# Shorter leads, a hand-written order of the last stage, and a last row added and normalised in another way, in a one-core kernel of two graph layers

## The reference, cut to what matters

```
N, F = 8192, 64                                     # adj is 8192 x 8192, float32 (268 MB)
x_drop = x * (u >= 0.1) / 0.9
x      = layernorm(x + adj @ x_drop)                # layer 1, rows of 64
proj   = tanh(|x|) * x / (|x| + 1e-8)               # row norms
s      = adj @ proj                                 # layer 2, the same adj
n      = clip(|s|, 0, 0.999)
out    = layernorm(x + (arctanh(n) * s / (n + 1e-8)) @ kernel + bias)
```

## Time and profile before

| | before |
|---|---|
| median of 3 runs | 947.8 us (947.53 to 947.82) |
| the profiled execution | 946.4 us |
| its span, first to last instruction | 944.2 us |
| PE busy | 898.7 us (95%) |
| DVE, POOL, ACT busy | 283.0, 56.9, 53.2 us |
| queue of the `adj`, `x` and `u` loads | 355.49 MB, 93.4% of the DMA engines' span |
| granted clock of TensorE, mean | 0.994 |

### The profile page before, as it was taken

One profiled execution on the slowest core, in us unless ns is written; L12 is line 12 of the kernel. 1 busy time (PEld: TensorE's weight loads), 2 busy tenths in 40 slices (PEclk: granted clock), 3 DMA queues, 4 the chain that ended last, 5 costly groups with the idle time before them and its releaser, 6 DMA issues.

```text
span 944.2 us, 10549 instructions
## 1 busy us (share of the span) xinstructions
PE 898.7 (95%) x4224; PEld 322.4 (34%) x4224; DVE 283.0 (30%) x1046; ACT 53.2 (6%) x138; POOL 56.9 (6%) x49
## 2 busy tenths in 40 slices
PE   5669999999999999999999999999999999999993
PEld 1113333333333333333333444444444444443331
DVE  1134574322314130304040221203121030336644
ACT  0000110000000000000000000000000000013322
POOL 0000000000000000000000000000000000003322
PEclk9999999999999999999999999999999999999997
DMA  9999999999999999997979998997989979899992
GB/s 369 414 421 420 421 421 420 421 422 421 421 421 421 421 417 422 380 423 258 424 237 413 390 363 320 341 423 283 407 290 370 422 269 362 336 423 421 421 422 108
DMA packets 53328, 358.35 MB, mean 380 GB/s; under 512 B 6305, under 2 KB 8353, under 8 KB 10401
## 3 DMA queue, kind: packets, MB, share of 16 engines
q1 hardware_dynamic: 50544, 355.49, 93.4%
q10 hardware_dynamic: 2736, 2.20, 0.7%
HBM read 355.57 MB, written 2.10 MB: 379 GB/s over the span
## 4 chain that ended last, share of the span: by engine, by line
PE 83%; DMA 7%; DVE 3%; SPq 2%; ACT 2%; POOL 1%; issue 1%; ACTq 0%; POOLq 0%; DVEq 0%
PE sums_both L629 38%; PE sums_first L583 20%; PE sums_part L592 16%; DMA ring<-adj_dram 7%; PE sums_part L583 4%; PE sums_both L611 3%; PE sums_part L611 3%; SPq L313 1%; ACT xres L363 1%; POOL rooted L330 1%; DVE stats L425 1%; SPq L309 1%; DVE y L541 1%; SPq L308 0%; DVE mv L428 0%
## 5 line engine op out<-in xcount | busy, mean ns | idle before, releaser
L629 PE MATMUL sums_both<-ring,feats 128*64 128x512 f32 x1696 | 370.3, 592 | 0.5 <-DMA ring<-adj_dram 0.5
L583 PE MATMUL sums_first<-ring,feats 128*64 128x512 f32 x1088 | 246.6, 599 | 28.4 <-DMA ring<-adj_dram 28.4
L629 PEld LDWEIGHTS sums_both<-ring,feats 128*64 128x64 f32 x1696 | 136.7, 137 | 228.0 <-issue 226.0
L592 PE MATMUL sums_part<-ring,feats 128*64 128x512 f32 x880 | 193.3, 593 | 0.0
L583 PEld LDWEIGHTS sums_first<-ring,feats 128*64 128x64 f32 x1088 | 78.8, 138 | 189.3 <-issue 140.1
L435 DVE TENSOR_TENSOR row_saved<-sums_both,row_saved 64x512 f32<-64x512 f32 x15 | 10.2, 683 | 349.3 <-ACT row_saved L383 349.2
L592 PEld LDWEIGHTS sums_part<-ring,feats 128*64 128x64 f32 x880 | 66.9, 137 | 119.0 <-issue 118.2
L340 POOL TENSOR_TENSOR rooted<-base,power 128x8 f32<-128x8 f32 x16 | 27.8, 1735 | 795.7 <-DVE base L462 795.7
L492 DVE TENSOR_TENSOR support<-sums_part,support 128x512 f32<-128x512 f32 x36 | 24.9, 692 | 139.2 <-PE sums_part L592 139.1
L583 PE MATMUL sums_part<-ring,feats 128*64 128x512 f32 x208 | 48.5, 595 | 2.8 <-DMA ring<-adj_dram 2.8
L383 ACT COPY row_saved<-sums_first 64x512 f32<-64x512 f32 x16 | 9.3, 580 | 600.4 <-PE sums_first L583 600.4
(11 more groups left out here) (64 smaller groups left out, 236.1 us busy)
## 6 DMA issues: line engine op xcount, KB each, us to landing
ring<-adj_dram SPq DMA_DIRECT2D x335, 1024.0 KB, 12.9
xres<-x_dram SPq DMA_DIRECT2D x8, 256.0 KB, 17.0
support<-u_dram SPq DMA_DIRECT2D x8, 256.0 KB, 16.8
out_dram<-xres ACTq DMA_DIRECT2D x16, 128.0 KB, 7.5
selw<-selector_dram ACTq DMA_DIRECT2D x1, 32.0 KB, 3.4
selw<-weight_dram ACTq DMA_DIRECT2D x1, 32.0 KB, 3.7
bias_sb<-bias_dram ACTq DMA_DIRECT2D x1, 32.0 KB, 6.1
```

The lines of the kernel that those rows point to most:

```text
L583: last = nc.tensor.matmul(bank[at:at + F], feats[:, c * TB + t, which, :], ring[:, slot, t, :], start=start and t < 2, stop=stop and t >= ...
L592: last = nc.tensor.matmul(bank[F * g:F * g + F], feats[:, c * TB + t, 1, :], ring[:, slot, t, :], start=start and t == 0, stop=stop and t ...
L629: last = nc.tensor.matmul(sums_both[r % 2][layer * F:layer * F + F], feats[:, c * TB + t, layer, :], ring[:, slot, t, :], start=begin and ...
```

## The change

It has these parts:

1. `LEAD` goes from 7 to 6. It counts in every row, and in the run of parts after the last row.
2. `EARLY_RUN` goes from 3 to 4: in row 1, `early` steps and steps of row 1 alternate in runs of four instead of three.
3. `HELD[2]` goes from 4 to 5: block (2, 6) is held and not read a second time. There are 334 loads instead of 335.
4. The order of the groups in the last stage is a list (`FINISHED`), and a second list (`GAPS`) says how many blocks stand between `finish` steps. The groups come in the same order as before. Some `finish` steps stand one or two blocks elsewhere.
5. For the last row (5), POOL clears the half of `support` that belonged to row 4 once row 4 was projected. VectorE then adds the whole 128 x 512 bank to it in one instruction, instead of two of 64 x 512, and the projection sums over 128 rows.
6. The last row's normalisation is shared: two of its four tiles on ScalarE as before, two on VectorE. Each half has its own store, from ACT's and from SP's queue.
7. `x` and `u` of a chunk come in one transfer of 512 KB instead of two of 256 KB, into a common tile `rows_in`. `support` shares the bytes of `u` as before.

```diff
-LEAD = 7
-EARLY_RUN = 3
-FINISH_EVERY = 3
-FINISH_LAG = 1
-HELD = [4, 4, 4, 3, 5, 4, 3, 4, 6, 5, 4, 3, 3, 2, 2, 1]
+LEAD = 6
+EARLY_RUN = 4
+HELD = [4, 4, 5, 3, 5, 4, 3, 4, 6, 5, 4, 3, 3, 2, 2, 1]
+FINISHED = [(14, 15), (12, 13), (8, 9), (10, 11), (0, 1), (2, 3), (6, 7), (4,), (5,)]
+GAPS = [7, 4, 4, 4.5, 4, 8, 5, 5, 5]
...
-            if ended and since >= FINISH_EVERY and now - ended[0][1] >= FINISH_LAG:
-                order.append(("finish", ended.pop(0)[0]))
-                since = 0
+            if ended < g and since >= GAPS[ended]:
+                order.append(("finish", groups[ended][0]))
+                ended, since = ended + 1, 0
...
-        xres = sb("xres", [P, NT, F])
-        support = sb("support", [P, NB // 2, BS])
+        rows_in = sb("rows_in", [P, 2, NT, F])
+        xres, keep = rows_in[:, 0], rows_in[:, 1]
...
-                    sp.dma_start(xres[:, t, :], x[:, t, :]).then_inc(chunk_loaded[chunk], 16)
-                    sp.dma_start(keep[:, t, :], u[:, t, :]).then_inc(chunk_loaded[chunk], 16)
+                    sp.dma_start(rows_in[:, :, t, :], xu[:, chunk]).then_inc(chunk_loaded[chunk], 16)
...
+                    if k == mate_done:
+                        pool.wait_ge(rows_projected, k + 1)
+                        nc.gpsimd.memset(support[half(final ^ 1), final // 2], 0.0).then_inc(mate_cleared, 1)
...
+                if k == len(groups) - 1:
+                    tiles = slice(final * TB, final * TB + TB // 2)
+                    for i in range(TB // 2):
+                        last = nc.scalar.activation(xres[:, final * TB + i, :], y_of[k % 2][:, i, :], ACT.Identity,
+                                                    scale=rooted[:, 0, i:i + 1], bias=shift[:, i:i + 1])
+                    last.then_inc(out_ready, 1)
+                    act.wait_ge(out_ready, rows_before(k) + 1)
+                    act.dma_start(out[:, tiles, :], xres[:, tiles, :]).then_inc(out_stored, 16)
...
-                if len(rows) == 2:
+                if n == final_part:
+                    dve.wait_ge(mate_cleared, 1)
+                if len(rows) == 2 or n == final_part:
                     total = support[:, rows[0] // 2]
                     V.tensor_tensor(total, bank[:], total, ALU.add).then_inc(part_added, 1)
...
+            dve.wait_ge(deviation_ready, 2 * k + 1)
+            for i in range(TB // 2, TB):
+                last = V.tensor_scalar(xres[:, final * TB + i, :], y_of[k % 2][:, i, :], mv[:, i, 0:1],
+                                       rooted[:, 0, i:i + 1], ALU.subtract, ALU.mult)
+            last.then_inc(final_halved, 1)
...
+                    for t in range(TB if rows == (final,) else 0):
+                        last = nc.tensor.matmul(projected[finished % 2][0][:, t, :],
+                                                support[:, final // 2, t * P:(t + 1) * P],
+                                                selw[:], start=True, stop=True)
```

More of the change, by code:

```diff
@@ L126, in work_order @@
     order += reread(LEAD, last) + column(last)
-    pairs = sorted(range(NB // 2), key=lambda p: 2 * NB - reread_to[2 * p] - reread_to[2 * p + 1])
     groups = []
-    for pair in pairs[:-1]:
+    for together in FINISHED:
         steps = []
         while True:
-            rows, low, high = behind(pair, NB)
-            if not rows:
+            low = min(reread_to[r] for r in together)
+            rows = tuple(r for r in together if reread_to[r] == low)
+            if low == NB:
                 break
+            high = min([NB] + [reread_to[r] for r in together if r not in rows])
             steps += partial(rows, range(low, high), False)
@@ L137, in work_order @@
                 reread_to[r] = high
[L138 to L144, removed]
+        groups.append((together, steps))
+    ended = since = 0
+    for g, (_, steps) in enumerate(groups):
         for step in steps:
             order.append(step)
-            now += len(step[1])
             since += len(step[1])
-            if ended and since >= FINISH_EVERY and now - ended[0][1] >= FINISH_LAG:
-                order.append(("finish", ended.pop(0)[0]))
-                since = 0
-        ended.append((rows, now))
-    for rows, _ in ended:
+            if ended < g and since >= GAPS[ended]:
+                order.append(("finish", groups[ended][0]))
+                ended, since = ended + 1, 0
+    for rows, _ in groups[ended:]:
         order.append(("finish", rows))
@@ L186, in place_blocks, with build @@
     return loads, uses
-def build(nc, adj, x, u, selector, weight, bias, out):
+def build(nc, adj, xu, selector, weight, bias, out):
     f32 = mybir.dt.float32
@@ L202, in build @@
     last_part = {r: s[3] for s in order if s[0] == "part" for r in s[1]}
+    final = groups[-1][0]
+    mate_done = next(k for k, rows in enumerate(groups) if final ^ 1 in rows)
+    final_part = last_part[final]
     def rows_before(k):
@@ L273, in build @@
         part_added = sem("part_added")
+        mate_cleared = sem("mate_cleared")
+        final_halved = sem("final_halved")
         root_asked = sem("root_asked")
@@ L313, in _ @@
                 sp.dma_start(ring[:, slot], adj[r, c]).then_inc(block_loaded[slot], 16)
+            tiles = slice(final * TB + TB // 2, final * TB + TB)
+            sp.wait_ge(final_halved, 1)
+            sp.dma_start(out[:, tiles, :], xres[:, tiles, :]).then_inc(out_stored, 16)
+            sp.wait_ge(out_stored, 16 * (NB + 1))
         @block.gpsimd
@@ L359, in normalise @@
                 act.wait_ge(deviation_ready, 2 * (k + 1))
+                if k == len(groups) - 1:
[6 more added lines that the diff above has]
+                    act.dma_start(out[:, tiles, :], xres[:, tiles, :]).then_inc(out_stored, 16)
+                    return
                 for g, r in enumerate(groups[k]):
@@ L401, in _ @@
                     k += 1
-            act.wait_ge(out_stored, 16 * NB)
+            act.wait_ge(out_stored, 16 * (NB + 1))
         @block.vector
@@ L417, in _ @@
                 t = slice(chunk * CHUNK, (chunk + 1) * CHUNK)
-                dve.wait_ge(chunk_loaded[chunk], 32)
+                dve.wait_ge(chunk_loaded[chunk], 16)
                 done(V.tensor_scalar(keep[:, t, :], keep[:, t, :], 0.1, 1.0 / KEEP_PROB, ALU.is_ge, ALU.mult))
@@ L573, in _ @@
                     k += 1
+            k = len(groups) - 1
+            dve.wait_ge(deviation_ready, 2 * k + 1)
[3 more added lines that the diff above has]
+            last.then_inc(final_halved, 1)
         @block.tensor
@@ L663, in _ @@
                         pe.wait_ge(projected_read, finished - 1)
-                    for t in range(TB):
+                    for t in range(TB if rows == (final,) else 0):
+                        last = nc.tensor.matmul(projected[finished % 2][0][:, t, :],
+                                                support[:, final // 2, t * P:(t + 1) * P],
+                                                selw[:], start=True, stop=True)
+                    for t in range(0 if rows == (final,) else TB):
                         for g, row in enumerate(rows):
@@ L685 @@
         "adj": np.ascontiguousarray(blocks),
-        "x": tiled(x),
-        "u": tiled(L0_gnn_u),
+        "xu": np.ascontiguousarray(np.stack([a.reshape(P, NT // CHUNK, CHUNK, F) for a in (tiled(x), tiled(L0_gnn_u))],
+                                            axis=2)),
         "selector": np.concatenate([np.eye(F, dtype=np.float32)] * 2),
```

2 lines of the change are left out of this document (1 added, 1 removed).

## The result

The changed kernel took 952.3 us (median of 5 runs, 951.5 to 953.1) against 947.8 before (median of 5 runs, 946.98 to 948.03): 1.0051 times as long, with a 95% interval of 1.0037 to 1.0065, or 4.5 us by the medians. Forecast were 950.9 us, slower, with a range from 946.0 to 953.2. So the two traces lie 5.5 us apart, one more than the medians.

A forecast was written before the change was run, and what follows sets the result against it. Loads were taken to bound the early stretch and last stage, PE the middle, then a serial closing chain. Terms 4.8 - 0.7 - 0.7 - 0.3 = +3.1 us on 947.8 gave 950.9 us, range 946.0 to 953.2.

The forecast's parts named there:

- What bounds which stretch: Loads set the pace to about 208 us, PE to the end of row 15 (816 us), loads in the last stage.
- The shorter lead: Six units (10.30 us) fall short of the way to `proj`; PE stops 0.4 us in 12 rows, 4.8 us.
- Rows 1 to 3: Early waits just use up 0.76 us of slack before load 77; only the wait for row 3 pays, 0.4 us.
- The closing chain: After the last block: one addition instead of two saves 0.7 us, the shared normalisation another 0.7 us.
- x and u in one transfer: Early stretch, where loads set the pace: merging transfers gives -0.3 us, bounds +0.3 and -1.3.
- FINISHED and GAPS: Last stage: loads hide any shift of PE's small waits up to 2.8 us; cost 0, bounds -0.3 and +1.
- The held block: One load less in the middle stretch, where slots are full: 0, with a price of no more than 0.3 us.
- hidden after all: Rival: the way to `proj` is covered, as only 0.34 us is missing; 946.1 us, chance 0.11.
- the number of loads: Rival: loads set the time, the saved load gives 2.5 us and PE gaps cost nothing; 943.6 us, chance 0.05.
- A dearer stop: Rival: PE restarts more slowly or waits at the earlier weight load, 0.8 us a stop; 955.7 us, chance 0.07.

The follow-up runs named there:

- held4: The changed kernel with HELD[2] back at 4, so one load more: 953.4 us, ratio 1.0064 to the kernel before.
- pad_lead6: The changed kernel with one more VectorE instruction (a copy of 128 x 256) in the way to `proj`: 957.6 us, ratio 1.0106 to the kernel before.
- lead7_rows: The changed kernel with a lead of 7 in the rows and still 6 in the last stage: 945.0 us, ratio 0.9982 to the kernel before.
- lead7: The changed kernel with LEAD back at 7 in the rows and in the last stage: 946.6 us, ratio 0.9995 to the kernel before.
- old_order: The changed kernel with LEAD, EARLY_RUN, HELD and the rule for `finish` steps of the kernel before: 945.2 us, ratio 0.9983 to the kernel before.
- old_finish: The changed kernel with the old rule for groups and `finish` steps in the last stage instead of the two lists: 956.9 us, ratio 1.0101 to the kernel before.

## Why the prediction was right, and where its size was off

*What bounds which stretch:* shown. A load more in the middle cost no 2.5 us (held4), a gap in PE there cost its length (pad_lead6), and the wait for row 15, in the last stage, cost nothing (lead7_rows).

*The shorter lead:* the mechanism was right, and it is the term of the sum that was mis-sized: 4.8 us forecast, 6.3 measured up to row 15's copy, beyond my upper bound of 5.8. The step that failed is "a wait of PE on VectorE ends 0.06 us after it". I had read that at a projection in the closing chain. At the parts of rows 4 to 14 it is 0.08 us at a single row's part and 0.23 at a pair's, with other waits beside it. Four of these rows are of the first kind, seven of the second. Against lead7, which stops at none of them, the copies fall behind by 0.43 us in each row of the first kind and by 0.59 in each of the second: from +1.00 us in row 4 to +6.82 in row 15, together 5.8, where I had 4.4. (Against before it is 6.26 - 0.66 = 5.6; lead7 itself gains 0.2 us on before there.) With those other waits out of the way the stop was the forecast one (0.39 us against 0.4).

*Rows 1 to 3:* the account came out. In the changed kernel PE reached load 77 with no stop and began its matmuls at 207.84 us, where the prediction had 207.79: the slack of 0.76 us was used up. Row 3's copy stood at +0.83 us. The wait for row 3 cost 0.6 instead of 0.4, and the kernel before spent its 0.76 on the wait for load 77 meanwhile, so row 4 stood at +0.83 + 0.6 - 0.76 = +0.66 where I had 0.4.

*The closing chain:* -1.4 us forecast (0.7 + 0.7), -1.4 measured in the changed kernel and in old_order (12.50 and 12.49 against 13.88 us). VectorE's half of the normalisation took 0.54 us for two tiles and was stored 0.5 us ahead of ScalarE's. POOL's clearing took 0.52 us, in idle time.

*x and u in one transfer:* -0.3 us forecast, -0.1 read in old_order, up to -0.4 in the other traces with a lead of 7, so the term is neither confirmed nor refuted. The Trainium skill gives a fixed part of about 2.0 us in each transfer issued from GpSimd (DMA: Bandwidth & Descriptors, Anatomy of one DMA). These transfers are issued from SyncE, and nothing of that size showed as a gain: eight transfers fewer moved the early stretch by 0.1 to 0.4 us.

*FINISHED and GAPS:* "cost 0" held for the sum, but only because part 1 and part 4 of the change belong together. I had argued that the loads hide any shift up to 2.8 us, without asking what the shorter lead in the last stage does under the old rule. There the lists are worth 4.0 to 4.6 us (956.9 against the changed kernel's 952.9 and 952.3). Under a lead of 7 they cost: lead7, with the lists, took 946.6 us and old_order, with the old rule, 945.2.

*The held block:* 0 forecast, and the measured difference (0.5 us for one load more, with overlapping intervals) doesn't contradict it.

Of the rivals, "hidden after all" and "the number of loads" are out (11 waits, held4). "A dearer stop" pointed the right way but not for its reason: in seven rows of eleven a stop came 0.17 us later than forecast (0.23 - 0.06), by the waits beside it and not by a slower restart or the earlier weight load, which would have been 0.4 us in every row. The forecast's range held the result with 0.9 us to spare at its upper end, although its bound for this term (5.8 us) didn't hold.

The sum with the measured terms is 6.3 + 0.8 - 1.4 - 0.2 = 5.5 us between the traces, of which the 0.8 is within what varied from execution to execution.

## What to carry to other kernels

Where work is put in front of a wait to cover a chain of other engines, measure both to a tenth of a microsecond: cover and chain were constants here, and 3% missing was paid in every row, while an excess of cover cost nothing. A table that was tuned for one lead is a table for that lead only; change them together or not at all. And read the delay of a wait at the place in question: a sole wait and one that stands with three others differed by 0.17 us here, which counts when it is passed seven times on the engine that sets the time.

## What the runs showed of the hardware that I had not expected

The delay from VectorE's last write to PE's weight load was 0.05 to 0.06 us with the wait alone or with that for a bank, 0.08 with those for one held block and a bank, 0.12 with those for two held blocks, and 0.23 with those for two held blocks and a bank. All those others had been met before.

After the stop of 5.7 us in old_finish the granted clock was at its lower level of 1.2 GHz for the projection, which took 2.08 us instead of 1.16:

```profile
875.00:881.40 6.40, 0.79 (x4) 0.00 (x0) 5.76 (x40) 1.21 (x4) 3.30 (x3) 0.73 1.02 419
881.50:883.50 2.00, 2.00 (x16) 1.79 (x16) 0.00 (x0) 1.66 (x6) 0.00 (x0) 0.50 1.01 426
```

From 883.5 to 885.0 us it was 0.59 in the mean, and 1.00 again from 885 to 887. The stops of up to 1 us at the leads left it at 1.00 (150 to 156, 254 to 260 and 294 to 300 us in the changed kernel).
